# Local layers of a gated transformer on one core: the transposes of queries and keys move ahead of two projections in TensorE's order

## The reference

```python
x = x + tanh(g_ffn[0]) * _L0_ffn_ref(_layernorm(x), ...)

for i in range(DEPTH):                      # DEPTH = 6
    x = attn_layer(shift_tokens(x), Wqkv[i], q_scale[i], k_scale[i], Wo[i]) + x
    x = ffn_layer(shift_tokens(x), ln_g[i], ln_b[i], W1[i], b1[i], W2[i], b2[i]) + x

def attn_layer(x, Wqkv, qs, ksc, Wo):       # 16 heads of 64, windows of 32
    q, k, v = split(x @ Wqkv, 3)            # each split into heads
    q = l2norm(q) * qs;  k = l2norm(k) * ksc
    q, k = rotated by cos/sin tables that carry a scale (xpos)
    out = local_attention(q, k, v)          # softmax over own and previous window
    return out @ Wo
```

## Time and profile before

| what | value |
|---|---|
| median of 3 runs | 2948.5 us (2945.0 to 2949.82) |
| the profiled execution's own time | 2950.04 us |
| its span, first to last instruction | 2948.3 us |
| mean granted TensorE clock | 0.951 of full |
| busy over the span | PE 2681.8 us (91%), PEld 1714.7 (58%), DVE 2078.4 (70%), ACT 1950.8 (66%), POOL 1638.5 (56%) |
| local layers in the trace | about 265 to 2060 us from the span's start |

### The profile page before, as it was taken

How to read it: one execution, slowest core, us unless ns; L and a number is a source line. 1 busy time by engine, 2 the same in 40 slices (tenths; PEclk the granted TensorE clock), 3 DMA queues, 4 the chain that set the end, 5 groups by cost and what they waited for, 6 DMA issues and landing times. The chain is left out here.

```text
span 2948.3 us, 69363 instructions
## 1 busy us (share of the span) xinstructions
PE 2681.8 (91%) x27218; PEld 1714.7 (58%) x27218; DVE 2078.4 (70%) x4018; ACT 1950.8 (66%) x5223; POOL 1638.5 (56%) x1893
## 2 busy tenths in 40 slices
PE   5996999999999999999999999998699888976995
PEld 2553766666666666666666666665244335542552
DVE  3674988888888888888888888885355335745763
ACT  3344888888888888888888888887233343544352
POOL 0522877777777777777777777775232004301520
PEclk8798999999999999999999999999799997998896
DMA  2001100010001000100010000000000000000000
GB/s 103 1 2 44 48 16 16 16 54 16 16 16 54 16 16 16 46 24 15 16 47 24 16 16 16 24 16 10 8 1 1 1 0 1 2 1 1 1 2 14
DMA packets 35645, 55.64 MB, mean 19 GB/s; under 512 B 7168, under 2 KB 32640, under 8 KB 33792
## 3 DMA queue, kind: packets, MB, share of 16 engines
q1 hardware_dynamic: 35328, 51.29, 5.7%
HBM read 25.05 MB, written 1.05 MB: 9 GB/s over the span
## 5 line engine op out<-in xcount | busy, mean ns | idle before, releaser
L1161 POOL TENSOR_TENSOR l_qk<-l_ta,l_tb 128x256 f32<-128x256 f32 x768 | 540.4, 738 | 285.2 <-DVE l_tb L1234 285.2
L675 POOL TENSOR_SCALAR qmr<-q_all,cf 128x256 fp32r<-128x256 f32 x128 | 116.0, 925 | 674.6 <-SPq L476 341.4
L707 DVE TENSOR_REDUCE mrow<-ring 128x2 f32<-128x512 f32 x512 | 324.5, 684 | 196.1 <-PE ring L523 183.9
L1057 ACT ACTIVATE l_pr<-st,l_mn 128x128 f32<-128x128 f32 x1152 | 354.9, 383 | 153.0 <-DVE l_mn L1220 153.0
L1177 POOL TENSOR_TENSOR l_qk<-l_qk,l_rn 128x512 f32<-128x512 f32 x384 | 392.6, 1044 | 102.6 <-DVE l_rn L1259 102.6
L1168 POOL TENSOR_TENSOR l_pr<-l_pr,l_rs 128x512 f32<-128x512 f32 x384 | 396.7, 1057 | 12.6 <-DVE l_rs L1249 12.6
L660 ACT ACTIVATE pt<-st 128x512 f32<-128x512 f32 x384 | 200.2, 600 | 288.0 <-PE st L558 288.0
L1238 DVE TENSOR_REDUCE l_sums<-l_sq 128x8 f32<-128x512 f32 x384 | 249.3, 659 | 27.6 <-ACT l_sq L1066 27.4
L548 PE MATMUL st<-qm,k_all 32*128 32x512 f32 x1024 | 222.8, 672 | 0.0
L1220 DVE TENSOR_REDUCE l_mn<-st 128x4 f32<-128x512 f32 x288 | 189.1, 685 | 41.2 <-PE st L918 38.8
L523 PE MATMUL ring<-ktr,qmr 32*128 32x256 f32 x1024 | 198.5, 396 | 13.8 <-POOL qmr L675 11.4
(11 more groups left out here) (232 smaller groups left out, 6438.9 us busy)
## 6 DMA issues: line engine op xcount, KB each, us to landing
l_vm<-l_v SPq DMA_DIRECT2D x192, 96.0 KB, 2.1
l_wa<-in_wa SPq DMA_DIRECT2D x6, 2048.0 KB, 9.4
l_vm<-l_v SPq DMA_DIRECT2D x192, 32.0 KB, 1.9
l_wf<-in_wf SPq DMA_DIRECT2D x6, 580.5 KB, 3.9
w<-in_w SPq DMA_DIRECT2D x1, 2752.0 KB, 15.8
cf<-in_cf SPq DMA_DIRECT2D x1, 1123.0 KB, 17.8
x<-in_xT SPq DMA_DIRECT2D x1, 1024.0 KB, 4.8
ctxT<-in_ctxT SPq DMA_DIRECT2D x1, 1024.0 KB, 8.3
```

The source lines that it names most:

```text
L707: dve.tensor_reduce(mrow[b % 2][:, t, j, 2 * p:2 * p + 2], bank_of(f"R{r}").rearrange("p (h k) -> p h k", h=2), AX.X, ALU.max).then_inc(ri ...
L1057: ins = act.activation(t.pr[:, u, hh, c, tile, :], bank(g, f"R{hh}", k)[:, x * P:(x + 1) * P], ACT.Exp, scale=-1.0, bias=t.mn[:, u, hh, x: ...
L1161: ins = pool.tensor_tensor(halves[0][:, :, x], halves[1][:, :, x], halves[2][:, :, 1 - x], ALU.add)
```

## The change

In TensorE's `step(N)`, the call of `turn(N+1)` is moved up by two places: from behind `project(N+2, 2)` and `project_back(N-2)` to directly behind `turn_probs(N-1)`. Nothing else is written differently, and the lists of the other four engines stay the same.

```diff
                 if 1 <= N <= STEPS:
                     turn_probs(N - 1, N - 1)
+                if 0 <= N + 1 < STEPS:
+                    turn(N + 1, N + 1)
                 if N >= 2 and N + AHEAD < STEPS:
                     project(N + AHEAD, 2)
                 if 2 <= N < STEPS + 2:
                     project_back(N - 2)
-                if 0 <= N + 1 < STEPS:
-                    turn(N + 1, N + 1)
                 if 2 <= N <= STEPS:
                     sum_values(N - 1, N - 1)
```

## The result

The changed kernel takes 3030.72 us (median of 5 runs, 3027.74 to 3036.31), the kernel before 2949.32 us (2945.0 to 2950.69). The ratio is 1.0278 (95% interval 1.0267 to 1.029): slower, by 81 us. The forecast was 3038 us with a range from 3021 to 3064.

A forecast was written before the change was run, and what follows sets the result against it. A ring through all engines (scores, minima, exponentials, copies, last part of `sum_values`) was taken to close each step; 67.8 + 3.7 + 4.8 + 12.8 = 89.1 us more gave 3038 us, range 3021 to 3064.

The forecast's parts named there:

- The wait and its place: TensorE's moved `turn`, reached at 2.70 in the step, stands still for all eight exponentials until 3.55, 0.85 us.
- the keys' wait: TensorE's wait at the last part of `sum_values` for ScalarE's copy of transposed keys, 0.36 us per step, goes.
- The chain of a plain step: TensorE's distances from `turn` at 3.55 to the next step, giving 8.43 us against 7.87, +0.56.
- The upper bound: First to last part of `sum_values` takes 1.02 instead of 0.72: 56 us more, 3094; near-1.02 rival, chance 0.05.
- Last part to scores: Distance on TensorE from the last part of `sum_values` to the start of the scores, taken as 0.39 us.
- the sum: Growth of all 188 moved-order steps, plain, mean square, center, pairs and down, together 89.1 us.
- The other kinds of step: Growth per step outside plain ones: mean square +0.56, center +0.16, pairs +0.22, down +0.58 us.
- The size of the wait: Idle before the transposes of line 899: 0.85 us, 188 times, some 160 us in all.
- VectorE's minima: VectorE's minima of the next scores were to wait for TensorE in every step, as a sign.
- The clock: Granted clock stays 1.00 in the local layers; rival that it falls: 92 us more, 3130, chance 0.04.
- The second ring: Ring through VectorE, GpSimd and refinement, called just as long as that through scores, minima, exponentials, copies and `sum_values`.
- the rival that had the change faster: Earlier `turn` feeds ScalarE earlier and TensorE's wait for the keys' copy goes without a new one: 2928 us, chance 0.03.

The follow-up runs named there:

- turn_before_back: Kernel before with `turn` moved up past the output projection only, staying behind the value projection; 2952.36 us, ratio 1.0008.
- turn_before_values: Kernel before with the order output projection, `turn`, value projection, so `turn` passes the value projection only; 2948.11 us, ratio 0.9996.
- after_no_sums: Changed kernel without the row sums taken along with the first four exponentials of a step (half replaced by ones); 2968.24 us, ratio to before 1.0056.
- before_no_sums: Kernel before without the row sums taken along with the first four exponentials of a step (half replaced by ones); 2922.11 us, ratio 0.9907.
- turn_in_first_bank: Changed kernel with the banks of turned queries and projected values exchanged, so `turn` waits for the first four exponentials only; 3035.35 us, ratio 1.029.
- queries_first_keys_last: Banks exchanged and `turn` cut in two: queries' half right behind the probabilities, keys' half directly ahead of `sum_values`; against kernel before 2957.03 us, ratio 1.0016.

## Why the prediction was right, and where it was off

**The wait and its place.** Right. `turn` stands still for the exponentials in 191 steps; the keys' wait is gone. turn_before_back and turn_before_values show that it takes both projections behind the wait, after_no_sums that the wait is what sets the time.

**The chain of a plain step.** It was put together from rows of before, most of them from the one step N = 1 that already had this order. Foretold and measured, in the step: `turn` 3.55 and 3.56, value projection 4.50 and 4.51, output projection 5.36 and 5.37, `sum_values` 6.32 and 6.33, last part 7.04 and 7.05. The upper bound, 1.02 from first to last part, did not hold, for the reason given.

**The term that was mis-sized.** Last part to scores: I took 0.39 from the earlier trace rows, where the last part starts behind a wait; it measures 0.33 (1096.05 to 1096.38) where it starts without one. In turn_before_back, where it still starts right at the keys' copy, it is 0.38 again. Over 188 steps 0.06 us are 11 us, and the sum with it is 78, against 80.0 measured in the stage and 81 for the whole.

**The other kinds of step.** Rows of the changed kernel that answer to the earlier trace rows, pairs (the step that starts at 1097.39, above) and down first, then center:

```profile
1104.77 1.12 PE L1002 MATMUL ring<-f_xn,l_wf 128*128 128x512 f32 x2
...
1111.12 1.98 PE L880 MATMUL st<-l_wa,l_xs 128*128 128x512 f32 x4
1115.01 1.11 PE L899 MATMUL st<-cf,l_qk 128*128 128x128 f32 x8 [1.03 <-ACT l_pr L1057]
1118.83 2.84 PE L1010 MATMUL st<-f_h,l_wf 128*128 128x512 f32 x6
1122.61 1.98 PE L880 MATMUL ring<-l_wa,l_xs 128*128 128x512 f32 x4
```

```profile
1147.76 1.98 PE L880 MATMUL st<-l_wa,l_xs 128*128 128x512 f32 x4
1155.14 1.12 PE L990 MATMUL st<-f_fs,cf 128*128 128x512 f32 x2
```

Pairs start at 7.38 (foretold 7.43, before 7.21), down at 7.71 (7.78, 7.20), center at 7.38 (7.43, 7.27). Each is off by the same 0.05 to 0.07 as the plain step. Center steps grow least, as foretold (0.11); down steps do not grow most but by 0.51, as plain and mean square steps do. Eight steps take 77.63 us instead of 74.28, 3.4 more and not 3.8. That center steps no longer wait for VectorE, which I had only argued, is what the row shows.

**The size of the wait.** I had said some 160 us in 188 waits of 0.85; it is 142.4 in 191. The start of `turn` was right; the profile draws the modelled end of the transposes ahead of it about 0.16 later than their distance says, so it shows 0.69 for 0.86. In the down steps it shows 1.03, since their exponentials end later.

**VectorE's minima.** I had written that they would wait for TensorE in every step. They do in 167. In the 22 down steps they start 0.49 behind the start of the step, before and after, behind VectorE's own feed-forward work. This did not touch the sum, since I had read the end of the exponentials of a down step (3.76) from such a step.

**The clock.** It stayed at 1.00 in the whole stage of 1832.9 us, with an idle time of about 0.7 us or more on TensorE in every step; what the earlier trace rows show for one step held for all. The Trainium skill ("TensorE: Matmul & The Clock Gate", section "A second HAM failure mode: psum-queue depth-cycling") tells of a kernel whose clock swung with small pauses between groups of matmuls; this trace shows no such swing at pauses of this size.

**The second ring.** This reading was wrong. The prediction called the ring through GpSimd and the refinement just as long as the first, since the refinement ended 0.05 before the minima. A short distance between two ends does not say which would move with the other. In before_no_sums plain steps fall to 7.68 us, and what stops them there is `turn` at 4.43 and the copies behind it; the refinement ends early enough for that in 88 of 97 steps. So there is a second limit close to the first, but it is TensorE's own list. The forecast did not depend on it, since the changed order starts `turn` at 3.55; it entered only the price of the rival that had the change faster.

**What stayed hidden.** The value and the output projection end later and nobody waits for them, as said. What I had not reckoned with is the second wait behind the first: the keys' half for ScalarE's first square, which turn_in_first_bank brought out. It sat in the measured 0.95.

## What to carry to other kernels

Before a waiting instruction is moved up in an in-order list, compare the time at which it will be reached with the time at which each of its waits is met, all of them: here 2.70 against 3.55 and, behind that, 4.04. Ask also whether the engine that it feeds is ready to take the result earlier: ScalarE was not here, and was only once its exponentials were 0.36 us shorter. Work that can run while another engine computes belongs ahead of such a wait, and one filler of the right length is enough; what exceeds the slack behind the wait lands on the ring. If the kernel anywhere runs the new order already, as in its first steps, that stretch gives the distances almost to the hundredth.

## What the runs showed that was not expected

- Eight short matmuls of 128x64 take 0.38 to 0.39 us to the next instruction if they start behind a wait and 0.33 if they follow others.
- The whole has a scatter of some 10 us from parts that no edit touched: queries_first_keys_last ran from 2945.11 to 2959.73 us, and in its profile of 2959.44 us the local layers took exactly what they take before. An edit of one stage is better judged by the windows of that stage.
